# Delta rule layer: the reciprocal roots of the norms computed as powers on GpSimd, and another order of work on five engines

## The reference

```python
mixed_qkv = hidden_states @ W_qkv
z = hidden_states @ W_z
beta = sigmoid(hidden_states @ W_b)
g = -exp(A_log) * softplus(hidden_states @ W_a + dt_bias)
q, k, v = split(silu(causal_conv(mixed_qkv, conv_w)))     # 8 key heads, 16 value heads, size 64
q = l2norm(q) * 64 ** -0.5                                 # x * rsqrt(sum(x * x) + 1e-6)
k = l2norm(k)
def step(S, (q_t, k_t, v_t, g_t, b_t)):
    S = S * exp(g_t)
    kv = k_t @ S
    S = S + outer(k_t, (v_t - kv) * b_t)
    return S, q_t @ S
o = o * rsqrt(mean(o * o) + 1e-6) * norm_w * silu(z)
return o @ W_out
```

## Time and profile before

| | |
|---|---|
| time, median of 3 runs | 2767.0 us (2761.95 to 2785.57) |
| profiled execution: its time, its span | 2778.46 us, 2776.8 us |
| busy in the span: PE, DVE, ACT, POOL | 79%, 68%, 52%, 28% |

### The profile page before, as it was taken

One profiled execution on the slowest core, in us unless ns is written; L12 is line 12 of the kernel. 1 busy time (PEld: TensorE's weight loads), 2 busy tenths in 40 slices (PEclk: granted clock), 3 DMA queues, 4 the chain that ended last, 5 costly groups with the idle time before them and its releaser, 6 DMA issues. The chain is left out here.

```text
span 2776.8 us, 63709 instructions
## 1 busy us (share of the span) xinstructions
PE 2194.6 (79%) x25656; PEld 1388.4 (50%) x25656; DVE 1890.6 (68%) x4429; ACT 1435.8 (52%) x2901; POOL 769.1 (28%) x845
## 2 busy tenths in 40 slices
PE   2698888889888493468888888888888886587984
PEld 1244444444444282146666666666666664365552
DVE  2477677777766325568888898888888883673433
ACT  0376667667666221255666666666666644132321
POOL 1000001000010141024444444344444442202884
PEclk8599899999887796668888988888888888597997
DMA  5000000000000042200000000000000000433334
GB/s 187 26 1 5 5 5 9 5 5 8 5 7 6 25 117 53 65 9 11 12 12 12 12 12 12 12 12 11 11 12 12 4 4 6 139 110 91 53 43 86
DMA packets 109526, 85.53 MB, mean 31 GB/s; under 512 B 22366, under 2 KB 97282, under 8 KB 108976
## 3 DMA queue, kind: packets, MB, share of 16 engines
q1 hardware_dynamic: 95664, 68.31, 8.4%
q0 software_dynamic: 13568, 13.14, 2.9%
HBM read 59.22 MB, written 22.71 MB: 30 GB/s over the span
## 5 line engine op out<-in xcount | busy, mean ns | idle before, releaser
L617 ACT ACTIVATE Pr<-Pr,nmax 128x512 f32<-128x512 f32 x512 | 341.2, 714 | 177.4 <-DVE nmax L552 175.3
L722 PE MATMUL bank<-ident,Pr 128*128 128x128 f32 x2048 | 315.5, 297 | 71.6 <-DVE PT L561 59.8
L722 PEld LDWEIGHTS bank<-ident,Pr 128*128 128x128 f32 x2048 | 242.1, 151 | 258.8 <-DVE PT L561 157.2
L552 DVE CUSTOM_DVE_ANT_0 Pr<-bank,Tb 128x512 f32<-128x512 f32 x512 | 331.0, 684 | 42.4 <-PE bank L708 42.3
L561 DVE COPY PT<-bank 128x512 f32<-128x512 f32 x256 | 176.4, 689 | 188.2 <-PE bank L736 184.0
L2431 PE MATMUL bank<-Wcv,hw 128*128 128x512 f32 x512 | 265.1, 665 | 8.8 <-POOL hw L1985 5.3
L2173 DVE TENSOR_TENSOR pr<-AC,Tc 128x30 f32<-128x30 f32 (+14 forms) x480 | 214.9, 448 | 16.9 <-POOL Tc L2049 3.6
L624 ACT ACTIVATE PT<-bank 128x512 f32<-128x512 f32 x256 | 151.0, 590 | 112.9 <-PE bank L736 83.3
L2174 DVE TENSOR_TENSOR Tc<-Tc,pr 128x30 f32<-128x30 f32 (+14 forms) x480 | 178.8, 373 | 16.5
L708 PE MATMUL bank<-kp,qp 8*128 8x512 f32 x1024 | 178.4, 696 | 1.1 <-DVE nmax L552 1.1
L2431 PEld LDWEIGHTS bank<-Wcv,hw 128*128 128x128 f32 x512 | 103.5, 214 | 125.8 <-issue 118.0
(11 more groups left out here) (398 smaller groups left out, 4533.6 us busy)
## 6 DMA issues: line engine op xcount, KB each, us to landing
aB<-alpha SPq DMA_DIRECT2D x64, 128.0 KB, 2.7
Tb<-scores SPq DMA_DIRECT2D x1, 7168.0 KB
w<-in_L_ffn_W SPq DMA_DIRECT2D x16, 256.0 KB, 5.2
rawW<-in_L_ffn_up_w SPq DMA_DIRECT2D x16, 256.0 KB, 3.1
rawW<-in_L_ffn_gw SPq DMA_DIRECT2D x16, 256.0 KB, 3.5
rawW<-in_L_ffn_down_w SPq DMA_DIRECT2D x16, 256.0 KB, 4.0
disp<-zero SPq DMA_DIRECT2D x1, 2580.0 KB, 15.5
xin<-disp SPq DMA_DIRECT2D x8, 322.5 KB, 6.3
```

What stands on the lines that cost most here:

```text
L552: V.tensor_tensor_reduce(out=Pr[:, s, i, :], in0=pS[hh][:, :], in1=Tb[:, h, at:at + L], scale=-1.0, scalar=3.0e38, op0=ALU.add, op1=ALU.mi ...
L617: A_(Pr[:, s, i, :], Pr[:, s, i, :], ACT.Exp, scale=-1.0, bias=nmax[:, s, i:i + 1])\
L722: last = TR(pT[m % 2][:, t * P:(t + 1) * P], Pr[:, (G % 2) * HG + hh, t, j * P:(j + 1) * P], ident[:, :])
```

## The change

- **Powers on POOL.** Constants of -0.5 stand in a third column of `eps`. For the output norms `inverse_root` on POOL scales and shifts `nrm` and raises it to the power -0.5 (tensor_tensor with ALU.pow, 16 elements a partition), and DVE's `scaled_norm` is left with the multiply. For q and k ACT only copies the sums (Copy in place of Sqrt), and `inverse_norms` on POOL adds the epsilons and takes the power of 32 elements. Both Sqrt of the loop and both reciprocals are gone.
- **Norms one step earlier.** PE, ACT and POOL do them at the end of the odd step; DVE's `norms` in the even step goes ahead of the first `conv`.
- **Output one step later.** PE and ACT do `output` in the step after, between the two `project`, and the loop has one more step.
- **Orders.** PE's second `add_state` goes behind the first `gate`. ACT's `weights(k, 0)` goes behind the second `project` in even steps. POOL's two `diag` and `weigh` change places so that `decay` and the first `diag` come first, then `inverse_root`. DVE's `scaled_norm` comes right after the second `conv`, and the piece of two rows of `substitute` ahead of `accumulate` in odd steps is gone (rows 12 to 17, 18 to 23, 24 to 30).

```diff
@@ MISC
-                if k % 2 == 0 and 0 <= k // 2 + 1 < NP:
-                    MISC += [("nm", k // 2 + 1)]
+                if 0 <= k - 2 < NS:
+                    MISC += [("out", k - 2)]
...
-                    MISC += [("ot", 2 * (k - 1)), ("ot", 2 * (k - 1) + 1), ("out", k - 1)]
+                    MISC += [("ot", 2 * (k - 1)), ("ot", 2 * (k - 1) + 1)]
+                if k % 2 == 1 and 0 <= k // 2 + 2 < NP:
+                    MISC += [("nm", k // 2 + 2)]
@@ gpsimd
+                    def inverse_root(k):
+                        pool.wait_ge(s["v_ss"], k + 1)
+                        G.tensor_scalar(nrm[:, k % 2, :], nrm[:, k % 2, :], 1.0 / DK, EPS1, ALU.mult, ALU.add)\
+                            .then_inc(s["g_ms"], 1)
+                        pool.wait_ge(s["g_ms"], k + 1)
+                        G.tensor_tensor(nrm[:, k % 2, :], nrm[:, k % 2, :], bcast(w["eps"][:, 2], 1, HV), ALU.pow)\
+                            .then_inc(s["g_or"], 1)
+
+                    def inverse_norms(m):
+                        pool.wait_ge(s["a_m"], done("nm", m))
+                        r = rkq[:, m % 3, :, :, :]
+                        G.tensor_tensor(r, r, bcast(bcast(w["eps"][:, 0:2], 1, 2), 3, HK), ALU.add).then_inc(s["g_re"], 1)
+                        pool.wait_ge(s["g_re"], m + 1)
+                        r = r.rearrange("p e w k -> p (e w k)")
+                        G.tensor_tensor(r, r, bcast(w["eps"][:, 2], 1, 4 * HK), ALU.pow).then_inc(s["g_rk"], 1)
@@ vector
-                    def inverse_norm(k):
-                        dve.wait_ge(s["a_or"], k + 1)
+                    def scaled_norm(k):
+                        dve.wait_ge(s["g_or"], k + 1)
                         n2 = nrm[:, k % 2, :].rearrange("p (k v) -> p k v", v=2)
-                        link(V.reciprocal(nrm[:, k % 2, :], nrm[:, k % 2, :]))
...
-                        dve.wait_ge(s["a_m"], done("nm", m))
-                        r = rkq[:, m % 3, :, :, :].rearrange("p e w k -> p (e w k)")
-                        link(V.reciprocal(r, r))
+                        dve.wait_ge(s["g_rk"], m + 1)
@@ scalar
-                    def roots(m):
+                    def norms(m):
...
-                            last = A_(rkq[:, m % 3, :, isq, :], bank[:, :, isq, :], ACT.Sqrt,
-                                      bias=w["eps"][:, isq:isq + 1], scale=float(DK if isq else 1))
+                            last = A_(rkq[:, m % 3, :, isq, :], bank[:, :, isq, :], ACT.Copy,
+                                      scale=float(DK if isq else 1))
```

More of the change, by code:

```diff
@@ L2055, in _ @@
                             window(k + 1)
+                        ahead = e == 0 and 0 <= m + 1 < NP
                         if 0 <= k < NS:
@@ L2207, in _ @@
                             read_out(k, 1)
+                        if ahead and e == 0:
+                            norms(m + 1)
                         if (k + 4) // 2 < NP:
@@ L2222, in _ @@
                             turn(m + 1)
-                        if past:
-                            inverse_norm(k - 1)
-                        if ahead and e == 1:
-                            substitute(m + 1, 18, 20)
                         if here:
@@ L2360, in _ @@
                             project(2 * (k + 4) + 1)
-                        if past:
-                            root_out(k - 1)
+                        if here and k % 2 == 0:
+                            weights(k, 0)
                         if 0 <= k + 1 < NS:
@@ L2381, in _ @@
                             turned(k - 1, 1)
-                            output(k - 1)
+                        if k % 2 == 1 and 0 <= k // 2 + 2 < NP:
+                            norms(k // 2 + 2)
                 @block.tensor
@@ L2545, in _ @@
                             read_out(k, 1)
-                        if ahead:
-                            norms(m + 1)
                         if (k + 4) // 2 < NP:
@@ L2570, in _ @@
                             gate(k, 0)
+                            add_state(k, 1)
                             gate(k, 1)
@@ L2574, in _ @@
                             turned(k - 1, 1)
-                            output(k - 1)
+                        if e == 1 and 0 <= m + 2 < NP:
+                            norms(m + 2)
             s.end()
```

47 lines of the change are left out of this document (25 added, 22 removed).

## The result

The kernel after takes 2811.7 us (median of 4 runs, 2800.7 to 2816.3) against 2770.5 us before in the same comparison: a ratio of 1.0118, with a 95% interval of 1.0084 to 1.0152. It is slower by 1.2%. The forecast was 2693, with 2645 to 2755 as its range. The profiled execution has a span of 2811.5 us, 34.7 more than before.

A forecast was written before the change was run, and what follows sets the result against it. The prediction took DVE to bound the kernel, with PE close. Gains of 8.1 us a pair less costs of 3.5 gave 4.6, over 16 pairs 74 us: 2693 us, with 2645 to 2755 as the 8-in-10 range.

The forecast's parts named there:

- DVE leads: Reading of the loop's bound: DVE hardly ever waits for a matmul, while PE waits 49.0 us for DVE's update of S.
- item 9: PE: `add_state` behind `gate` frees 3.3 us a pair; norms ahead of the read-out slow the clock; 1.0 charged.
- Item 5: DVE's reciprocals disappear: 0.8 us a pair gained.
- Item 7: POOL's new powers, scales and adds hold DVE: 0.65 us lost in odd steps, 0.3 in even ones.
- Item 8: POOL's two `weigh` operations in odd steps now run beside `substitute` on DVE: 1.3 us a pair lost.
- item 2: ACT's second `project` no longer waits for `solve`, so DVE's wait for `yp` goes: 2.8 us a pair gained.
- Item 3: POOL builds Lt beside DVE's PSUM adds, so the scan's wait for it goes: 1.0 us a pair gained.
- Item 4: POOL's multiply of S no longer runs beside DVE's scan: 1.6 us a pair gained.
- Item 6: DVE's multiply of `nrm` no longer held: 0.8 us a pair gained in odd steps, 0.4 taken back.
- Item 1: Norms a step earlier: DVE's wait for Sqrt goes, 1.5 us a pair gained; a new wait for POOL's power put at zero.
- the wait moves to PE: Rival: PE at 1.2 GHz before the read-out becomes the leader, gain stops at 2.5 us a pair, 2727 us; chance 0.19.
- slow-power rival: Rival: POOL's power takes many microseconds; 3.7 us a pair lost per us above 1.9, 2930 us at 5 us; chance 0.09.

The follow-up runs named there:

- run 6: Kernel after with Sqrt and reciprocals as before (no powers), and the q and k norms back at their old places on PE, ACT and DVE: 2718.6 us, 0.9801.
- run 2: Kernel after with all its orders, but Sqrt on ACT and reciprocals on DVE as before, no power on POOL: 2762.0 us, 0.9955 of before.
- run 11: Kernel before with one edit, PE's second `add_state` moved behind `keys` and the first `gate`: 2733.9 us, 0.9838.
- run 10: run 2 with only DVE's norms back behind `total`; those of PE and ACT stay ahead of the read-out: 2744.1 us, 0.991 of before.
- run 1: Kernel after with both powers on POOL replaced by multiplies by 1e-6: 2790.6 us, 1.0054 of before.
- run 4: Kernel after with only the output norms' power replaced by a multiply, the 32-element power kept: 2792.8 us, 1.0065 of before.
- Run 12: Kernel before with one edit, ACT's `weights(k, 0)` of even steps moved behind the second `project` and `root_out`: 2775.9 us, 1.0.
- run 14: run 6 with ACT's `weights(k, 0)` of even steps back ahead of the second `project`, as before: 2735.8 us, 0.9875 of before.
- run 15: Kernel after with PE's second `add_state` back ahead of `keys`, as before: 2803.5 us, 1.0102 of before.
- run 16: run 1 with ACT's `weights(k, 1)` of odd steps moved behind the first `squash`: 2773.6 us, 1.0005 of before.
- run 17: run 6 with the output norms as a power on POOL, and ACT's `weights(k, 1)` of odd steps behind the first `squash`: 2732.0 us, 0.987 of before.
- run 18: Kernel after with ACT's `weights(k, 1)` of odd steps moved behind the first `squash`: 2792.4 us, 1.0045 of before.

## Why the prediction was wrong

Two steps of the prediction failed, and a third had the wrong size. The first is "DVE leads": the waits of DVE and PE were counted as gains that add, and they are largely one stall. The second is "PE is done with the norms before it starts `project`, `output` and the read-out", with its price of 1.0 in item 9: the read-out came late, and the move cost 43 us. The third is the roots on POOL, items 5, 7 and 8: the mechanism was right, and the loss that I forecast is half of the measured one.

In three parts, in us a pair (a pair is taken as a sixteenth of the difference in time):

| part | forecast | measured |
|---|---|---|
| orders, without the moved norms (items 2, 3, 4, 6 and its 0.4) | 5.8 gained | 3.45 gained (run 6) |
| norms moved (items 1 and 9, freed waits of `add_state` counted in) | 0.5 gained | 2.65 lost (run 2 against run 6) |
| roots on POOL (items 5, 7, 8) | 1.45 lost | 2.85 lost (after against run 2) |
| sum (the forecast less 0.25 of rounding) | 4.6 gained | 2.05 lost |

How the miss divides between the first two lines depends on where the freed waits of `add_state` (3.3) are booked. Run 6 has the late `add_state` too; with its gain moved up, the first line would read 9.1 forecast and the second 2.8 lost, as measured, and nearly the whole miss of the two would be that the gains didn't add. Run 11, `add_state` alone, has 2.8 of the 3.45.

The steps from run 6 to the kernel after add up the loss, in per cent of before: from 0.9801, norms ahead of the read-out on PE and ACT +1.1 (run 10), DVE's norms ahead of `conv` +0.45 (run 2), roots on POOL at no length instead of on ACT and DVE +1.0 (run 1), the length of the long power +0.1 (run 4), that of the short one +0.5: 1.0118. The steps of 0.1 and 0.45 are within the noise.

- **"DVE leads."** This reading failed first. DVE and PE had 60.7 and 60.5 us of work a pair, and I took PE's 49.0 us of waits for DVE as the mark of a follower. They are two engines in a ring, each waiting for the other in its turn. Run 11 touched only PE's order and gained 45 us, and the waits of the earlier trace rows, 75.1 us over the stretch of its list, were 35.3 in it.
- **Items 1 to 3, the waits, 5.3 us a pair.** As single causes they were wrong. Run 12 removed the cause of item 2 and gained nothing. Its edit became a gain (0.7%, run 14) only with PE in time. Item 3's wait for Lt stayed, 14.6 us: I covered the first `diag`, but the second still stands behind power and `weigh`, and the scan waits there instead (1.00 us at 1699.06).
- **Item 4, the scans,** came out as sized: 25.9 us for 26.3. **Item 5,** too. **Item 6:** the multiply of `nrm` fell by 30.4 us, but `substitute` waits 4.1 us for Tc in the stretch, not 1 to 2 a pair; DVE waits at that place for `add_state` instead (3.46 us at 1707.37).
- **Item 1's second half and item 9.** "PE is done with the norms before it starts `project`, `output` and the read-out" was true and the wrong way round: the read-out is now late by them. I had the numbers in item 9, norms of 4.01 us and `project` at half speed, and let the freed waits of `add_state` pay for all but 1.0 us a pair. PE's wait for S did go, but others of 83.7 us in sum came (see the result). Run 10 against run 6 puts the place on PE at 30 us, 1.9 a pair, and run 15 shows that the freed waits, which were to pay for it, are worth nothing in that company, where run 11 shows them at 45 us, 2.8 a pair. With its DVE half the move costs 43 us, as much as the roots on POOL (45). Run 6, which has neither, is 55 us faster than before; that this is not far from the 74 of the forecast is luck, since the forecast counted both as small. The rival "the wait moves to PE" named it, with a gain left over at its end. It had the right place and too small a price.
- **`norms` ahead of `conv` on DVE,** which I priced at zero, are held by `decay`, which runs right then (`gk` took 1.94 us at 1687.58, beside POOL's S at 1687.57, 1.90): 41.7 us for 8.8, 2.1 a pair.
- **Item 7, the power.** 2.97 and 5.43 us, where the bounds were 0.16 to 1.91: half again above the upper end. The bound, 64 passes over the data, was no bound, since nothing ties a function to the price of passes. Its consequence was smaller than the slope in the slow-power rival said: 3.7 us a pair for each us above 1.9 would be 4 us a pair, and both lengths together cost 18 us, 1.1 a pair (after against run 1), most of it in the short one. That rival's sum at 2.97 us, 2.7 a pair or 43 us slower, lies near the 33 measured by luck: by it the kernel with short powers is faster than before, and run 1 is not. Of the signs of being wrong, the powers above 1.9 us and the longer `substitute` came; `norms` waits for POOL once only, and PE works 61.0 us a pair at 0.87.
- **Item 8** had the right mechanism, named before: Ws comes early because ACT is free, and Ud and `decay` leave `conv` for `substitute`. Its size was off, 1.3 us a pair where `substitute` alone lost 44.7 us, 2.8 a pair.
- **The port rule.** The Trainium skill, page "SBUF — State Buffer", section "Who interferes with whom", has the ports that DVE and GpSimd share as an exclusive lock, for which a DVE operation with two inputs in SBUF contends with a GpSimd one that reads SBUF. For Ud and S this trace agrees, 4.25 us for 1.2. For the power, which reads SBUF too, it doesn't: DVE's operations with two inputs in SBUF took 0.41 us beside it. The measurement decides, and it fits that the 182 us of powers did no more harm.
- **The ends.** I took the start as equal and left 2 us of gain in the rounding. The start is 6.4 us longer, 5.4 of it by the norms' place (run 2 has it too), and the loop's last steps are 2.8 longer; in the last of them the power (2.9 us at 2372.46) stands in the open.

What stays open: the 28 us between runs 1 and 2, of which run 16 may account for 14 (the late Ws was not tried on runs 2 and 6, and it might gain there as well), and why ACT comes late for the `gate` in the kernel after, where the gain of `add_state` vanishes. That the late read-out is behind it is argued from runs 11 and 15 and was not tried by itself.

## What to carry to other kernels

Where two engines are both near 90% busy and wait for each other, a wait belongs to the ring and not to the edge on which the trace books it: try each order edit alone, since here one was worth 1.6%, another nothing, and all of them together 0.45%. Don't put work ahead of the operation with which the other engine's step begins, least of all the norms here, 32 matmuls of two columns, behind which the granted clock was 0.50. And before an engine is relieved, look at what it will start earlier and beside whom: here a multiply on POOL was free beside DVE's PSUM work (1.07 us in the earlier trace rows) and cost DVE most of its length beside work on two SBUF inputs (3.0 us for 4.5).

## What the runs showed that I had not expected

- POOL's power takes about 0.15 us for each element of a partition, 2.97 us for 16 and 5.43 for 32, against 1.27 for the multiply of 512 in `gated`. It doesn't hold a DVE operation with both inputs in SBUF (0.41 us beside it), where multiplies do.
- A later start of one 0.6 us copy on ACT made three kernels faster, by 0.5, 0.6 and 0.7% (runs 16, 17, 18). The first two alone are hardly clear of noise, but in all three traces `substitute` is 11 to 19 us shorter.
- DVE's copy of 32 elements from SBUF to SBUF, `rkd`, is held as well: a mean of 1.13 us in the kernel after against 0.17 before, though it has one input only.
